# The last addition of a cycle, moved behind the second unit's maxima in VectorE's order

## What is computed

```python
scores = jnp.einsum('bqhk,bshk->bhqs', Q, K) / jnp.sqrt(d_head)
attn = jax.nn.softmax(scores, axis=-1)
out_h = jnp.einsum('bhqs,bshk->bqhk', attn, V)
return jnp.einsum('bqhk,hdk->bqd', out_h, W_O) + b_O
```

## Time and profile before

| | us |
|---|---|
| median of three runs | 3922.62 |
| lowest, highest | 3916.49, 3926.24 |
| the profiled execution, its own time | 3927.83 |
| its span in the profile | 3925.9 |
| PE busy | 3653.8 (93%) |
| DVE busy | 2896.5 (74%) |
| ACT busy | 2270.9 (58%) |

### The profile page before, as it was taken

One profiled execution on the slowest core, in us unless ns is written; L12 is line 12 of the kernel. 1 busy time (PEld: TensorE's weight loads), 2 busy tenths in 40 slices (PEclk: granted clock), 3 DMA queues, 4 the chain that ended last, 5 costly groups with the idle time before them and its releaser, 6 DMA issues.

```text
span 3925.9 us, 67314 instructions
## 1 busy us (share of the span) xinstructions
PE 3653.8 (93%) x25781; PEld 1931.0 (49%) x25781; DVE 2896.5 (74%) x5821; ACT 2270.9 (58%) x2635; POOL 11.1 (0%) x17
## 2 busy tenths in 40 slices
PE   4999999999999958999999995699999999999997
PEld 2445445454554425555555554245545455554544
DVE  5777878778787676777777765477777877778784
ACT  3666666666666515655655652466666666666663
POOL 1000000000000000000000000000000000000000
PEclk9999999999999979999999997899999999999998
DMA  1000000000000000000000000000000000000000
GB/s 51 7 9 10 9 12 7 9 10 9 9 8 8 8 13 7 15 15 12 15 12 13 11 15 3 19 7 12 8 9 10 10 9 10 9 10 8 7 9 17
DMA packets 44405, 44.40 MB, mean 11 GB/s; under 512 B 16466, under 2 KB 30554, under 8 KB 43834
## 3 DMA queue, kind: packets, MB, share of 16 engines
q1 hardware_dynamic: 44090, 40.09, 3.4%
HBM read 37.56 MB, written 1.70 MB: 10 GB/s over the span
## 4 chain that ended last, share of the span: by engine, by line
PE 79%; DVE 11%; issue 5%; ACT 4%; DMA 1%; SPq 1%; DVEq 0%; ACTq 0%
PE ps L558 75%; DVE over L1231 2%; DVE acc L1211 2%; DVE wexp L1231 1%; DVE x L1369 1%; ACT Kh L986 1%; ACT work L1014 1%; PE ps L877 1%; PE ps L888 1%; DVE Kd L1154 1%; PE ps L547 1%; DVE stats L1123 1%; PE ps L917 0%; SPq L468 0%; SPq L436 0%
## 5 line engine op out<-in xcount | busy, mean ns | idle before, releaser
L1014 ACT ACTIVATE work<-ps 128x1024 f32<-128x1024 f32 (+1 forms) x1344 | 1277.0, 995 | 957.2 <-PE ps L558 953.0
L1211 DVE TENSOR_TENSOR acc<-acc,work 128x1024 f32<-128x1024 f32 (+2 forms) x1152 | 1352.0, 1174 | 47.3 <-ACT work L1014 11.5
L558 PE MATMUL ps<-work,V 128*64 128x512 f32 (+3 forms) x5376 | 1234.8, 579 | 0.0
L558 PEld LDWEIGHTS ps<-work,V 128*64 128x64 f32 x5376 | 450.7, 137 | 539.5 <-issue 444.2
L558 PE MATMUL ps<-Qh,Kh 64*128 64x512 f32 (+3 forms) x2688 | 652.9, 481 | 26.1 <-issue 10.6
L1231 DVE CUSTOM_DVE_ANT_0 over<-ps,over,mpart 128x512 f32<-128x512 f32 (+3 forms) x642 | 422.6, 696 | 309.3 <-PE ps L558 309.2
L558 PE MATMUL ps<-Qh,Kl 64*128 64x512 f32 (+3 forms) x2688 | 526.0, 385 | 0.0
L558 PE MATMUL ps<-Ql,Kh 64*128 64x512 f32 (+3 forms) x2688 | 522.6, 383 | 0.0
L558 PE MATMUL ps<-auxQ,auxK 64*128 64x512 bf16 (+3 forms) x2688 | 518.5, 380 | 0.0
L1231 DVE CUSTOM_DVE_ANT_0 wexp<-ps,wexp 128x512 f32<-128x512 f32 (+1 forms) x632 | 377.0, 636 | 29.8 <-PE ps L558 29.8
L558 PE MATMUL ps<-Kh,Qh 64*128 64x512 f32 (+2 forms) x1520 | 350.7, 467 | 34.1 <-DVE mpart L1231 13.0
(11 more groups left out here) (187 smaller groups left out, 2541.3 us busy)
## 6 DMA issues: line engine op xcount, KB each, us to landing
rden<-inverse_sums SPq DMA_DIRECT2D x192, 128.0 KB, 2.9
auxQ<-mrow SPq DMA_DIRECT2D x384, 1.0 KB
wqk<-in_wqk SPq DMA_DIRECT2D x24, 128.0 KB, 2.4
dcomp<-rden SPq DMA_DIRECT2D x192, 2.0 KB
wv<-in_wv SPq DMA_DIRECT2D x24, 64.0 KB, 2.2
inverse_sums<-rcomp SPq DMA_DIRECT2D x96, 4.0 KB, 1.3
work<-in_mlp_w SPq DMA_DIRECT2D x1, 1024.0 KB
work<-in_c_aux SPq DMA_DIRECT2D x1, 1024.0 KB, 4.9
```

The lines of the kernel that those rows point to most:

```text
L558: return pe.matmul(o, w, m, start=start, stop=stop, skip_group_check=True)
L1014: act.activation(work[:, 2 * e:2 * e + 2, q0:CH], ps[:, b:b + 2, q0:CH], ACT.Exp, scale=L.scale).then_inc(s["p_ready"], 1)
L1211: dve.tensor_tensor(o, o, work[:, slots[two]:slots[two] + 2, q0:CH], ALU.add).then_inc(s["acc_ready"], 1)
```

## The change

VectorE's order at the beginning of a cycle changes. Before: the first unit's maxima, the last addition of the preceding cycle, in layer 2 the maximum of tile 0 where a new pair begins, the second unit's maxima. After: the first unit's maxima, the maximum of tile 0, the second unit's maxima, the last addition. No instruction is added or taken away, and the other engines' orders and waits are the same.

```diff
                     for sl, m, u in before_:
-                        if sl == 0:
-                            tops(m, u)
+                        if sl == 1 and L.tile0_in(x) is not None:
+                            tops(m, 0)
+                        tops(m, u, slot=sl)
                     for which in last:
                         add(*which)
-                    if L.tile0_in(x) is not None:
-                        tops(L.tile0_in(x), 0)
-                    for sl, m, u in before_:
-                        if sl == 1:
-                            tops(m, u, slot=1)
                     for m, c in L.due(L.mul_at, x):
                         normalise(m, c)
```

## The result

The kernel after takes 3995.34 us (median of six runs, 3991.45 to 3996.28), the kernel before 3923.3 us (six runs, 3916.49 to 3933.4): the ratio is 1.018 with a 95% interval from 1.0169 to 1.0191. That is +72 us, where +68 were forecast.

What follows compares the result with a forecast made beforehand. TensorE, busy 93% of the span, was taken as the bound, so VectorE's order counts only where TensorE waits for it. The terms 39 + 31 + 4 - 6 = +68 us gave 3991 us, range 3950 to 4016 us.

Steps and rivals of the forecast that it cites:

- output projection: `op` cycles of layers 0 and 2: later `normalise` delays TensorE's projection, which has little or no slack; +39 us.
- rows of the maxima: Chunk beginnings in layers 0 and 2: later `mval` and `mrow` delay the first score product through SyncE's DMAs; +31 us.
- sums: 75 `den` cycles: the product with `ones` waits for the later last addition, between nothing and 0.4 us; +4 us.
- earlier maxima: Second maxima come 0.36 us earlier, freeing TensorE 18 us before `excess`; about 6 us left, most in layer 1.
- A: Rival: faster, TensorE waits for the second maxima before `excess`; 3905 us, or down to 3808 us; chance 0.04.
- B: Rival: no change, both delay and gain are hidden, within 3911 to 3934 us; chance 0.03.
- C: Rival: only one of the two chains, projection or maxima's rows, costs; 3945 to 3965 us; chance 0.15.
- D: Rival: more than the sum, VectorE's delay isn't used up at the next first maxima; 4005 to 4035 us; chance 0.18.

Runs made afterwards that it cites:

- experiment 1: Kernel after, but in layers 0 and 2 `normalise` goes ahead of the last addition: 3953.72 us, ratio 1.0084.
- experiment 2: Kernel after, but with the old order in the `mt` cycles of layers 0 and 2: 3959.38 us, ratio 1.0097.
- experiment 3: Kernel after, but with the old order in the `op` and `mt` cycles of layers 0 and 2: 3918.73 us, ratio 0.9988.
- experiment 4: Kernel after, but with the new order in layer 1 alone and the old one in layers 0 and 2: 3913.36 us, ratio 0.9981.
- experiment 7: Kernel after, but in layers 0 and 2 the new order only in the inverse's cycles, not `op`, `mt` or `den`: 3910.85 us, ratio 0.997.
- experiment 5: Kernel after, but in steady cycles of layers 0 and 2 `normalise` also goes behind the cycle's first addition: 4101.82 us, ratio 1.0461.

## Why the prediction was right, step by step

| step of the prediction | forecast, us | measured, us | by |
|---|---|---|---|
| output projection | +39 | +41.6 | experiment 1 |
| rows of the maxima | +31 | +36.0 | experiment 2 |
| sums | +4 | +5 to +8, where the rows are in time | experiments 3, 4, 7 |
| earlier maxima | -6 | -10, a part of it the clock | experiment 4 |
| kernel after | +68 | +72 | the result |

The measured terms add up to 73 us with the lower figure of the sums and to 75 us with the upper one, against 72 us.

*The mechanism* was right in both halves. The second maxima became earlier, waited 307.9 us for TensorE (200 or more was forecast), and gave nearly nothing in layers 0 and 2, because ScalarE held the next step; what followed them came later, and the releases without slack passed this on. The projection stood 0.15 us behind `normalise` in every steady cycle of layers 0 and 2 (0.14 was forecast).

*Output projection.* Measured from the end of the product ahead of it, its start moved by 21.6 us in layer 0 and 19.7 us in layer 2, summed over 30 projections each (20.6 and 18.8 forecast); 20.0 and 17.9 us of this are visible idle time. The release is as late as was worked out; the slack of 0.12 and 0.19 us was taken some 0.03 us too large in each cycle. In layer 0 the usual distance before is 0.25 us, not the 0.28 us of the row that was read.

*Rows of the maxima.* By kind of chunk, experiment 2 gives for layer 0, net of what the sums then cost: first 0.69, second 0.30, third 0.63, fourth 0.70 us. The forecast had 0.61 (10.9 / 18, the beginnings that stall already), 0.28, 0.60 and 0.59. The second chunk, which gives back part of the delay, came out as read from the earlier trace rows. The fourth is undersized by 0.11 us, the largest miss among the kinds.

*Sums.* This term was sized too small. The forecast let the addition release TensorE 0.05 us after its end; in experiments 2 and 3 the product with `ones` begins 0.15 us behind it in the `den` cycles of layer 0. From the waits of experiment 2:

```profile
PE ps L558 <- DVE acc L1211: 3.1, 14, 0.5
```

Measured from the end of the product ahead of it, that product begins later than before by 4.7 us in sum in layer 0 and 2.5 us in layer 2. This makes 7.2 us, near the 7.9 us between experiments 3 and 7. The `den` cycles of layer 0 show the same: they are 0.03, 0.28, 0.21 and 0.04 us longer in experiment 2 than before. In layer 1, whose sums are among the 75 of the forecast, no cycle became longer. In the kernel after the term is mostly hidden: there the late rows have delayed TensorE already in the same cycle, and the product with `ones` begins only 1.4 us later in sum. So the 36.0 us of experiment 2 are what was left of the rows' price once the sums had come out.

*Earlier maxima.* The gain in layer 1 was undersized. Four of its ten cycles became shorter, by 0.15, 0.34, 0.34 and 0.18 us: 1.0 us for a pair, 8 us in all. The forecast had 7.2 us freed there, and after what is swallowed again 6 us for all three layers. TensorE waits there for the last maxima before `excess`. Before, with the idle time of TensorE in brackets:

```profile
1826.42 0.44 PE L558 MATMUL ps<-Kd,Qh 64*128 64x384 f32 x2 [1.01 <-DVE mpart L1231]
```

and after, in the same cycle of the pair:

```profile
1867.20 1.22 DVE L1211 TENSOR_TENSOR acc<-acc,work 128x1024 f32<-128x1024 f32 x1
1867.34 0.19 PEld L558 LDWEIGHTS ps<-Kd,Qh 64*128 64x128 f32 x2 [0.86 <-DVE mpart L1231]
1867.34 0.44 PE L558 MATMUL ps<-Kd,Qh 64*128 64x384 f32 x2 [0.68 <-DVE mpart L1231]
```

The addition now begins when the maxima are done, and TensorE's wait is 0.33 us shorter. This is the one place where the change does what its form suggests, and it is why experiment 4 is faster than before.

*The rivals.* A (the second maxima are what TensorE waits for) holds in layer 1 alone, for 8 to 10 us. B (no change) is out by the result. C (only one chain costs) is out, since each of experiments 1 and 2 removes its own term and experiment 3 removes both. D (the delay isn't used up at the next first maxima) is out: the cycles that follow an `op` cycle, those with `mt`, are as long as before to 0.05 us, and those with the inverse, which follow `den`, to 0.02 us. Nor is there a further price of the stalls themselves: the `op` cycles of layer 0 became 0.68 to 0.80 us longer, no more than the 0.68 to 0.84 us by which the projection's start moved in nearly all of them.

Part of the nearness is luck: the misses of the two chains and the sums, +2.6, +5 and +1 to +4 us, were partly met by a gain 4 us larger than forecast, some of which is the clock's.

## What to carry to other kernels

On an engine that works through a written order, moving an instruction ahead is worth only what its own successor had to wait for, and it costs every instruction that now stands behind it. So for each thing that comes later, measure the distance from its end to the start of its user, and look for the shortest such distance: one at 0.15 us, or one that equals the distance where the user visibly stalls, has no slack, even where the trace shows no idle time. The same edit can have opposite signs in stages with different limits, so it is to be priced stage by stage: here +37 and +42 us in the layers with full tiles and -10 us in the causal one.

## What the runs showed of the hardware

**A short idle time of TensorE can halve its clock for some 3 us.** In experiment 5 the granted clock is 0.50, its 1.2 GHz level, in a stretch behind an idle time of 1.95 us, and the busy time of layers 0 and 2 rises by 25 us. The trace's clock has 16 such stretches behind their first cycles, nine in layer 0 and seven in layer 2, for 60 such idle times, so not each one brings it; at about 1.7 us each (5.33 - 3.63) they make up the rise. None of the other nine traces has one there. In after the idle times of 0.61 and 1.41 us shown above brought none; the mean clock of layer 0 stayed 1.00. Layer 1 of the kernel before has four such stretches. Two windows around each of two of them, the first of each pair ahead of it:

```profile
1605.00:1609.00 4.00, 2.55 (x40) 1.99 (x39) 4.00 (x17) 2.61 (x4) 0.00 (x0) 1.00 0.00 0
1609.20:1612.40 3.20, 3.18 (x24) 2.54 (x26) 2.99 (x4) 1.02 (x1) 0.00 (x0) 0.50 0.02 6
2039.00:2042.00 3.00, 1.62 (x28) 1.39 (x28) 3.00 (x12) 1.58 (x3) 0.00 (x0) 1.00 0.00 0
2042.60:2045.80 3.20, 3.20 (x24) 2.14 (x24) 2.64 (x3) 1.72 (x3) 0.00 (x0) 0.50 0.13 39
```

They stand behind the 1.01 us wait shown above, which has shorter waits ahead of it, in a cycle that takes 11.3 us without and 12.8 to 12.9 us with such a stretch. After has two of them, and experiment 4 none. So of the 13.7 us that layer 1 gained in experiment 4's trace, some 8 us come from the order and 6 us from the clock. The nine traces with the new order in layer 1 have none to two such stretches each in its steady cycles, against four in the one trace of before: that the order brings fewer is likely, not shown. In which of equal cycles the clock falls is left open.

**The issue of small DMAs lies on the way of the data.** SyncE issues the four DMAs of one set of rows in 2.56 us, one behind another; with two on each of two queues the way from `mrow` to the score product shrinks from 3.67 to 2.56 us, although the bytes are the same.
